# Row 0's selector and chosenT spread over 128 rows, and a padded last half of Wo, in a transformer layer on one Trainium2 core

## The reference

```python
xn = _layernorm(x)
q, k, v = heads(xn @ Wq.T + bq), heads(xn @ Wk.T + bk), heads(xn @ Wv.T + bv)
q, k = rope(q), rope(k)
att = softmax(where(tril, q @ k.T / sqrt(16), -inf))
attn = (att @ v) @ Wo.T + bo
prob = softmax(xn @ router_w.T + router_b)        # 16 blocks
mask = one_hot_of(top_k(prob, 4))
h = relu(where(mask, xn @ w1.T + b1, 0))          # mask spread over blocks of 64
out = x + attn + (h @ w2.T + b2)
```

## Time and profile before

| | |
|---|---|
| median of 3 runs | 824.03 us (823.89 to 825.13) |
| the profiled execution | 824.19 us |
| its span, first to last instruction | 822.3 us |
| TensorE matmul busy | 799.8 us (97%), 4923 instructions |
| VectorE busy | 615.2 us (75%) |
| ScalarE busy | 410.3 us (50%) |
| GpSimd busy | 336.9 us (41%) |

### The profile page before, as it was taken

How to read it: one execution, slowest core, us unless ns; L and a number is a source line. 1 busy time by engine, 2 the same in 40 slices (tenths; PEclk the granted TensorE clock), 3 DMA queues, 4 the chain that set the end, 5 groups by cost and what they waited for, 6 DMA issues and landing times.

```text
span 822.3 us, 14185 instructions
## 1 busy us (share of the span) xinstructions
PE 799.8 (97%) x4923; PEld 461.1 (56%) x4923; DVE 615.2 (75%) x1880; ACT 410.3 (50%) x858; POOL 336.9 (41%) x348
## 2 busy tenths in 40 slices
PE   7999999999899999999999999999999999999998
PEld 3666454444455555555655655555666556465664
DVE  6858978878999777686897967768587878768423
ACT  3513544655364565445463554545365463546462
POOL 4485058515740165639324127636802013022120
PEclk9999999999999999999999999999999999999999
DMA  8952516332334544242150636133060443310021
GB/s 261 267 167 78 155 33 180 114 92 92 86 135 110 137 138 150 80 116 91 44 170 17 163 105 180 67 110 105 35 195 26 107 116 105 84 41 15 2 71 52
DMA packets 66147, 88.11 MB, mean 107 GB/s; under 512 B 7324, under 2 KB 34972, under 8 KB 66076
## 3 DMA queue, kind: packets, MB, share of 16 engines
q1 hardware_dynamic: 66076, 87.21, 36.4%
HBM read 49.22 MB, written 37.98 MB: 106 GB/s over the span
## 4 chain that ended last, share of the span: by engine, by line
PE 81%; POOL 5%; DVE 5%; ACT 5%; issue 3%; DMA 1%; SPq 0%; ACTq 0%; DVEq 0%; POOLq 0%
PE o_bank L1250 15%; PE banks L1158 12%; PE banks L1170 12%; PE banks L1142 12%; PE banks L1232 12%; PE banks L1116 7%; ACT probs L1043 4%; PE banks L1125 3%; PE banks L1197 3%; DVE banks L1448 2%; PE banks L1236 1%; POOL pieces L896 1%; POOL hT L904 1%; PE banks L1147 1%; DVE banks L1457 1%
## 5 line engine op out<-in xcount | busy, mean ns | idle before, releaser
L1043 ACT ACTIVATE probs<-banks 128x512 f32<-128x512 f32 (+1 forms) x608 | 311.9, 580 | 280.6 <-PE banks L1236 112.8
L1232 PE MATMUL banks<-q_st,k_st 99*128 99x512 bf16 (+3 forms) x768 | 208.5, 327 | 5.8 <-ACT probs L1043 3.7
L1170 PE MATMUL banks<-k_st,q_st 96*128 96x512 bf16 (+3 forms) x768 | 211.8, 327 | 2.0 <-DVE row_max L1448 1.5
L1445 DVE TENSOR_REDUCE part_max<-banks 128x1 f32<-128x512 f32 x256 | 160.2, 678 | 12.0 <-PE banks L1170 11.5
L1448 DVE CUSTOM_DVE_ANT_0 banks<-banks,tri,part_max 128x512 f32<-128x512 f32 (+3 forms) x256 | 128.7, 555 | 54.0 <-PE banks L1170 53.6
L1142 PE MATMUL banks<-xnT,w_sb 128*128 128x256 f32 x512 | 135.7, 388 | 1.6 <-ACT probs L1043 0.7
L1448 DVE CUSTOM_DVE_ANT_0 banks<-banks,tri 128x512 f32<-128x512 f32 (+3 forms) x256 | 119.2, 512 | 20.4 <-PE banks L1170 20.0
L1250 PE MATMUL o_bank<-probs,v_sb 128*17 128x512 f32 (+3 forms) x1536 | 133.4, 487 | 0.0
L904 POOL TENSOR_TENSOR hT<-hT,gates 128x512 f32<-128x512 f32 x48 | 55.5, 1158 | 180.5 <-ACT hT L1029 152.2
L1158 PE MATMUL banks<-w_sb,hT 128*128 128x256 f32 x512 | 122.5, 383 | 2.6 <-POOL hT L904 1.8
L1232 PEld LDWEIGHTS banks<-q_st,k_st 99*128 99x128 bf16 x768 | 69.1, 97 | 77.7 <-ACT probs L1043 27.3
(11 more groups left out here) (100 smaller groups left out, 746.8 us busy)
## 6 DMA issues: line engine op xcount, KB each, us to landing
term_scratch<-pieces SPq DMA_DIRECT2D x84, 256.0 KB, 2.9
q_st<-term_scratch SPq DMA_DIRECT2D x16, 768.0 KB, 6.0
k_st<-term_scratch SPq DMA_DIRECT2D x16, 768.0 KB, 8.6
y_scratch<-o_norm SPq DMA_DIRECT2D x31, 256.0 KB, 2.5
gates<-gate_scratch SPq DMA_DIRECT2D x24, 256.0 KB, 6.3
acc<-in_x SPq DMA_DIRECT2D x8, 512.0 KB, 4.0
rope_sb<-y_scratch SPq DMA_DIRECT2D x15, 256.0 KB
out<-acc SPq DMA_DIRECT2D x7, 512.0 KB, 2.9
```

The lines of the kernel that those rows point to most:

```text
L1043: nc.scalar.activation(probs[:, h:h + shared(k), PROBS_AT[u]:PROBS_AT[u] + w], bank, ACT.Exp, scale=SCALE).then_inc(s_out, 1)
L1170: nc.tensor.matmul(bank[:, 0:w], q_st[0:KROWS, at, h, i * P:(i + 1) * P], k_st[0:KROWS, at, h, c * HALF:c * HALF + w], start=True, stop=Tr ...
L1232: last = nc.tensor.matmul(bank[:, i], k_st[0:SROWS, at, h + i, j * P:(j + 1) * P], q_st[0:SROWS, at, h + i, q0:q0 + w], start=(i == 0), st ...
L1445: ins = nc.vector.tensor_reduce(part_max[:, h, at:at + 1], bank[:, 0:w], AX.X, ALU.max)
```

## The change

`sel` and `chosenT` get 128 partitions in place of 16, so that the penalty's matmul contracts over 128 rows; rows 16 to 127 of both are zero. `chosenT` is filled once by GpSimd, ahead of its other fills, and the copy of VectorE still writes 16 rows. The waits on `ones_set` count one higher. For the last half batch, the second matmul of `last_out_rest` contracts over all 128 rows of `yT[:, 1]` with `wo_half`, whose lower 64 rows are zero; the values of group 14 are loaded a second time so that the lower rows hold numbers. `wo_half` comes with `wo_last` in one load, and its wait moves ahead of these matmuls. SP stores the last four tiles one by one.

```diff
-        wo_last = x_sb[:, 0, :]
-        sel = gates[0:NBLK, 1, 0:FB // 2, :].rearrange("p a (c m) -> p (a c) m", m=P)
+        wo_last, wo_half = x_sb[:, 0, :], x_sb[:, 1, :]
+        sel = gates[:, 1, 0:FB // 2, :].rearrange("p a (c m) -> p (a c) m", m=P)
-        chosenT = sb("chosenT", [NBLK, T], BF16)
+        chosenT = sb("chosenT", [P, T], BF16)
...
-                sp.dma_start(gate_scratch[b % 2], chosenT[:]).then_inc(chosen_out, 16)
+                sp.dma_start(gate_scratch[b % 2], chosenT[0:NBLK, :]).then_inc(chosen_out, 16)
...
-            def load_y(b, c, first, stop):
+            def load_y(b, c, first, stop, at=None):
...
-                at = first % 2 * GH * HD
+                at = first % 2 * GH * HD if at is None else at
...
-                    sp.dma_start(wo_last, wo_last_c).then_inc(wo_last_in, 16)
+                    sp.dma_start(x_sb[:, 0:2, :], wo_last_c).then_inc(wo_last_in, 16)
...
                     load_y(b, 1, 2, 3)
+                    load_y(b, 1, 2, 3, P // 2)
             store_out(B - 1, 0)
-            for u in range(2, 4):
-                sp.wait_ge(m_out, M_COUNT["outl", 2 * u + 1])
-                t = slice(2 * u, 2 * u + 2)
+            for t in range(NT // 2, NT):
+                sp.wait_ge(m_out, M_COUNT["outl", t])
                 sp.dma_start(out_rows[B - 1, :, t, :], acc[:, t, :]).then_inc(stored[1], 16)
             sp.wait_ge(stored[0], B * 16)
-            sp.wait_ge(stored[1], (B + 1) * 16)
+            sp.wait_ge(stored[1], (B + 3) * 16)
...
+            nc.gpsimd.memset(chosenT[:], 0.0).then_inc(ones_set, 1)
             nc.gpsimd.memset(v_sb[:, :, :, :, HD:VW], 1.0).then_inc(ones_set, 1)
...
                 if t == NT // 2:
-                    pe.wait_ge(y_in[1], B * Y_INC)
+                    pe.wait_ge(y_in[1], B * Y_INC + 16)
+                    pe.wait_ge(wo_last_in, 16)
...
-                nc.tensor.matmul(bank[:, 0:D], yT[0:P // 2, 1, tokens], wo_sb[0:P // 2, 1, :], start=False, stop=False)
+                nc.tensor.matmul(bank[:, 0:D], yT[:, 1, tokens], wo_half, start=False, stop=False)
...
-                if i == 0:
-                    pe.wait_ge(wo_last_in, 16)
...
-                if b == 1:
+                if b == 0:
+                    dve.wait_ge(ones_set, 1)
+                elif b == 1:
                     dve.wait_ge(s_out, S_COUNT["hid", 0, 3, FB - 1])
-                elif b:
+                else:
                     dve.wait_ge(chosen_out, (b - 1) * 16)
-                nc.vector.tensor_copy(chosenT[:], bank.bitcast(BF16)[0:NBLK, :]).then_inc(m_out, 1)
+                nc.vector.tensor_copy(chosenT[0:NBLK, :], bank.bitcast(BF16)[0:NBLK, :]).then_inc(m_out, 1)
...
-    sel = np.zeros((NBLK, FB, P), np.float32)
+    sel = np.zeros((P, FB, P), np.float32)
...
-    arrays["wo_last"] = wo_last.reshape(P, D)
+    wo_half = np.zeros((P, D), np.float32)
+    wo_half[:P // 2] = arrays["woT"][P:P + P // 2]
+    arrays["wo_last"] = np.stack([wo_last.reshape(P, D), wo_half], axis=1)
```

More of the change, by code:

```diff
@@ L947, in _ @@
             pool.wait_ge(xn_ready, NT)
-            pool.wait_ge(ones_set, 1)
+            pool.wait_ge(ones_set, 2)
             nc.gpsimd.memset(k_st[KROWS:P, :, :, :], 1.0).then_inc(ones_set, 1)
-            pool.wait_ge(ones_set, 2)
+            pool.wait_ge(ones_set, 3)
             pool.wait_ge(bias_in, 16 * 5)
@@ L955, in _ @@
             nc.gpsimd.tensor_tensor(bo_sb[:], bo_sb[:], b2_sb, ALU.add).then_inc(ones_set, 1)
-            pool.wait_ge(ones_set, 3)
+            pool.wait_ge(ones_set, 4)
             add_biases(0, 0)
@@ L1061, in _ @@
                 if what == ("v", 0, 0):
-                    act.wait_ge(ones_set, 1)
+                    act.wait_ge(ones_set, 2)
                 if what == ("hid", 0, 0, 0):
@@ L1289, in _ @@
                 work(what)
-            pe.wait_ge(ones_set, 2)
+            pe.wait_ge(ones_set, 3)
             for what in STEPS:
@@ L1481, in normalise @@
                 if n == 0 and c == 0:
-                    dve.wait_ge(ones_set, 3)
+                    dve.wait_ge(ones_set, 4)
                 link(nc.vector.transpose(o_bank[:], o_bank[:]))
```

## The result

| | before | after |
|---|---|---|
| median | 824.0 us | 814.99 us (814.82 to 816.43) |
| ratio | | 0.9892, 95% interval 0.9877 to 0.9907 |
| profiled execution, span | 824.19, 822.3 | 814.86, 812.9 |

A forecast was written before the change was run, and what follows sets the result against it. TensorE was taken to set the pace. Row 0's 7.2 us less 0.6 gave 6.6, plus 1.5 in the tail: 8.1 us off, predicting 815.9 us, range 813.5 to 818.9.

The forecast's parts named there:

- The pause around small matmuls: Row 0's hidden blocks: time lost right before and after the 16-row selector matmul; 1.27 us a block should become 0.97.
- the signs: Expected in the profile after: selectors 0.97 us apart, no weight loader pause ahead, first maxima near 43.8, tail pitch 0.43.
- 8.1 lost, 0.9 of it stays: Row 0's 32 selector blocks: 8.1 us lost to pauses, 0.9 stays as exposed weight loads, 7.2 us remain to win.
- The seven blocks behind a pause or a short matmul: Row 0 blocks not following a selector: their first f32 weight load stays exposed, keeping 7 x 0.10 us.
- the four half covered ones: Row 0's four blocks at 1.22 us: first weight load half covered, keeping 4 x 0.05 us.
- How it builds up: Row 0's gain by stage: 2.3 us by 46.1, 1.6 more by 68, 1.7 by 103, 1.6 up to 186.
- I charge 0.6 us: Row 0, where VectorE is nearly full: an earlier TensorE only waits longer; 0.6 us of gain lost, between 0.2 and 3.0.
- the full stretches: Row 0, 58 to 68 and 94 to 107 us: VectorE nearly full, so TensorE's gain might be lost there.
- First stack, selector's load, fill: Start of the kernel: stack lands with 0.6 us to spare, larger selector load and 0.9 us GpSimd fill covered; cost 0.
- The tail: Last half batch: eight padded Wo matmuls win 1.56 us; with the stores 1.5 us, bounds 1.2 and 1.8.
- The stores: Tail's four single stores on SP: last transfer of 128 KB lands in 2.1 us, not 2.2; last issue up to 0.3 late.

The follow-up runs named there:

- the drags: Four VectorE reductions, two in each of row 0's two full stretches, added to the changed kernel (817.91 us) and to the kernel before (825.67 us).
- sel_96rows: The changed kernel with the selector's matmul contracting over rows 0 to 95 only: 815.4 us, ratio 0.9887 to the kernel before.

## Why the prediction was right, step by step

- **The pause around small matmuls.** Right, and that the rows are its cause is shown: 16 and 64 rows pay it, 96 and 128 don't, whatever the type, the place in the group, or the number of small matmuls in a row. Predicted 0.97 a block, measured 0.98 and 0.97. Of the signs, the loader's idle time is gone too.
- **8.1 lost, 0.9 of it stays.** Right. In the changed kernel's timeline the 32 blocks take 32.2 us where they took 39.2: 7.0 won, 7.2 predicted. The seven blocks behind a pause or a short matmul still take 1.08 and the four half covered ones 1.02 to 1.04, as the term had it.
- **How it builds up.** Less the 0.25 of the start: 2.3 at the first maxima (2.3 predicted), 3.9 at quarter 2 (3.9), 5.25 at its last block (5.4), 7.0 at the last block of all (7.0).
- **"I charge 0.6 us".** This term was mis-sized. 0.15 was lost by 96 us, and was back by 177. The mechanism exists, as the drags show: VectorE can hold TensorE up there. But the pauses ahead of the full stretches sufficed, as far as the traces tell. I also read one stretch as too long: VectorE is full from 93.9 to 105.3, not to 107; then it idles the 2.36 us ahead of 107.64, and 0.44 of the gain went there. VectorE's idle time between the first maxima and the end of the row fell by 4.1 us, from 28.4 to 24.3, where I had said about 5. Its window, columns as in the earlier trace rows:

```profile
43.70:199.40 155.70, 153.09 (x931) 86.65 (x930) 131.40 (x406) 74.67 (x150) 82.60 (x78) 1.00 0.38 113
```

- **First stack, selector's load, fill.** Costed at 0; no row shows a wait for them. The stack landed 0.4 ahead of its need, not 0.6. The load took 5.2 us to land in place of 4.3. The fill took 0.95 us (0.9 predicted) and left GpSimd 3.65 us of idle time ahead of the norm's power:

```profile
0.72 0.95 POOL L941 MEMSET chosenT<- 128x1024 bf16 x1 [0.29 <-POOLq L1638]
...
5.81 1.04 POOL L947 TENSOR_TENSOR rstd<-var,half 128x4 f32<-128x4 f32 x1 [3.65 <-DVE var L1348]
```

- **The tail.** 1.56 predicted, 1.57 measured at the adds (9.10 less 7.53), though the parts differ a little: 0.1 less at the first matmul, 0.1 more in the last group (0.63 from its start to the first add, 0.74 before), whose first load is now covered. The stores were mis-sized: I counted them as 0.1 won and 0.15 lost, and they gave 0.24, since 128 KB landed in 1.8 us and not in 2.1, with SP 0.1 behind.

The 1.2 us between the forecast and the profiled execution are 0.6 of that charge, 0.3 of the stores, and 0.25 of the start, which no edit made; 0.1 more came from waits of the later batches.

## What to carry to other kernels

Look for matmuls on 64 rows or fewer among others on 96 to 128: here the pause shows as idle time of the weight loader that nothing releases, 0.33 us each time, and zero rows took it away for one fill and a longer load. Count changes, not matmuls; two small ones in a row paid once. Before you count on a gain of the engine that sets the pace, look for pauses of the engine that follows ahead of the place where it is full, not only at its idle time on average. This last advice rests on the reading above, which no run tested.

## What the hardware showed beyond that

The changed kernel's one execution at 816.43, 1.3 to 1.6 above its others, has a granted clock of 0.998. In sel_96rows such an execution was profiled, at 816.16 with 0.998, where its fastest took 814.95. Two windows of it and the same two of the changed kernel's profiled execution, columns as in the earlier trace rows:

```profile
210.00:214.00 4.00, 2.69 (x11) 1.30 (x10) 3.97 (x12) 0.60 (x1) 3.70 (x6) 1.00 0.46 121
214.00:218.00 4.00, 4.00 (x28) 1.10 (x30) 3.28 (x15) 1.79 (x6) 0.27 (x2) 0.57 1.03 264
```

```profile
210.00:214.00 4.00, 2.69 (x11) 1.31 (x10) 3.96 (x12) 0.61 (x2) 3.66 (x6) 1.00 0.47 127
214.00:218.00 4.00, 3.80 (x40) 1.44 (x39) 3.59 (x16) 1.78 (x6) 0.22 (x1) 1.00 0.99 253
```

In both, TensorE is busy 2.69 of 4 us while VectorE is full. In sel_96rows the granted clock of the next 4 us is 0.57, so mostly at the lower level, 1.2 GHz; the changed kernel's execution kept 2.4 GHz. From 203 to 223 the slower one falls 1.3 us behind and stays there: the `pv` matmuls of 214.96 take 3.5 us until the next start, those of 214.88 in the other 2.3. So the same thin stretch can be followed by either level of the clock, and in this execution that cost 1.3 us, where the tail's whole gain is 1.8. Whether this is also the cause in executions that weren't profiled isn't shown.
